# Routed experts in units of two tiles and one, with a row list summed from one-hot tiles

## The chip, the cores and the metric
The kernel runs on one core of a Trainium2 chip. The metric is the device time of one execution in microseconds; the median of three runs before the change is 2113.64 us (2112.92 to 2113.86).

## What is computed
A block of two layers on x of 1 x 2048 x 512 in float32. Layer 0 is a recurrent time mixing, multiplied by the silu of a feed-forward with 2 experts of which each token takes one; layer 1 is a grouped attention (16 heads, 4 key heads, remote keys pooled in blocks of 64, the last 256 kept), multiplied by the silu of a mixture of experts: two shared ones and the best 4 of 16 routed ones for each token. The part that the change touches:

```python
# attention of layer 1
probs = jax.nn.softmax(scores, axis=-1)
out = jnp.einsum('bhqk,bhkd->bhqd', probs, v2)
# mixture of layer 1
scores = jax.nn.sigmoid(flat @ centroids.T) + bias
vals, idx = jax.lax.top_k(scores, KR)                      # KR = 4 of 16
gating = jnp.zeros_like(scores).at[jnp.arange(T)[:, None], idx].set(vals)
gating = gating / jnp.clip(gating.sum(-1, keepdims=True), 1e-08)
hj = jax.nn.relu(flat @ w1 + b1)                           # per expert, 512 -> 352
yj = hj @ w2 + b2                                          # 352 -> 512
acc + yj * g[:, None]
```

## The kernel before
The program is a row of stages, each a block in which the five engines run their own instruction streams and meet by semaphores; between two stages all engines meet. Every product is made in three passes: an operand is kept as a high part (fp32r, cast by ScalarE) and a low part (the rest, subtracted by VectorE or POOL), and TensorE sums high x high, low x high and high x low (`PASSES`). In order of time the stages from layer 1 on are the shared experts with the router, keys and values, window, routed experts, attention.

**Shared experts and router** (`shared_experts_stage` L172, `top4_router` L1587). Eight steps k (two experts x four blocks of 512 tokens). TensorE runs hidden(k), the router's piece of the step, then down(k-1). POOL subtracts the low half of the hidden tiles (L229). VectorE adds the results to y (L272) and runs the router: scores, rank and gates in steps 0 to 3, the places of the tokens in the sorted order (`places`, L1681) in step 4, the shares (L1704) in step 5. From step 5 on POOL scatters (`scatter`, L1770): the 2048 x 4 choices are 64 columns of 128 tokens, and one indirect DMA writes one column of token numbers to their places in the list `idx` in device memory, 32 of them in this stage.

**Keys and values** (`keys_values_stage` L2076). POOL clears the key tiles (L2164), then adds the rotated halves of the keys of block b (L2169), and after each of the four adds scatters eight more columns. VectorE subtracts the weights' low half (L2221), multiplies for the rotation (`rotate`, L2231 and L2232), pools the keys (L2237), and prepares the pooled keys (L2265). TensorE runs `geo_block` 0 and 1, the values, `geo_block` 2 and 3 (L2291), and then places the pooled keys with narrow matmuls of 32 columns (L2325). SP loads raw_o and raw_q, weights of the attention output and query, for the next stage.

**Window** (`window_stage` L2343). Eight units u of window attention. VectorE: `shift(u)` (maxima, L2628), `probs_low(u-1)` (low halves of the turned probabilities, L2662 and L2667), `inverse(u)` (sums and reciprocals, L2644 to L2655). ScalarE: `exps(u)`, `probs_high(u-1)`, `probs(u)`. TensorE: `turn(u)`, then `scores(u+2)`, and `attend` behind every second.

**Routed experts** (`routed_experts_stage` L1789). The sorted list is cut into MT = 47 units of 256 rows (MR), each of one expert. The units run in a loop of two (`tiles`, L1842). SP loads a unit's w1 (two raw buffers) and w2 (one raw buffer, `raw2`) and stores the result y. POOL copies the unit's two columns of indices (L1900), adds on a carrier (L1903), gathers two tiles of 128 rows (L1905) and subtracts w1's low half (L1911). ScalarE casts the high halves (w1 L1936, x L1941, w2 L1950), makes the relu from PSUM into `h32` (L1956) and casts the hidden tile (L1959). VectorE subtracts w2's low half (L1985), the hidden tile's (L1988), the rows' (L1970), and copies y (L1978). TensorE in each unit: 36 hidden matmuls of 256 columns (L2036), 8 transposes of the next unit's rows (L2009), 18 matmuls of the down product of the unit before (L2019). At the stage's start the index list is loaded, turned on TensorE (L2025) and copied by VectorE (L1980) before the first gather.

**Attention** (`attention_stage` L2817). One step of each engine's stream per tile n of 128 queries. TensorE:

```python
if n < NR: geo_query(n)
if 0 <= n - 1 < NR: turn_q(n - 1)
if 0 <= n - 2 < NR: turn_p(n - 2)      # transposes of the probabilities, L3103
if 0 <= n - 1 < NR: scores(n - 1)      # L3113, L3117, then L3122
if 0 <= n - 2 < NR: output(n - 2)      # L3132
```

`turn_p` waits for VectorE's normalised probabilities (att_p, L3016), which follow its maximum (att_mx, L2999) of the scores of that tile.

## Time and profile before

| | |
|---|---|
| median of three runs | 2113.64 us |
| profiled execution, its own time | 2117.64 us |
| its span, first to last instruction | 2115.8 us |
| mean granted clock of TensorE | 0.921 |
| TensorE / VectorE / ScalarE / POOL busy | 85% / 58% / 39% / 49% |
| shared experts and router | 1048.0 to 1238.2 us |
| keys and values | to 1313.5 us |
| window | to 1448.4 us |
| routed experts | to 1911.9 us |
| attention | to 2115.8 us |

Times are microseconds from the span's start. The busy shares are means over stages with different limits, so a stage is read by its own stretch. A matmul's duration reaches beyond the start of the next one, since they overlap; the distance of two starts tells the rate. "[3.39 <-POOL shared_h1l L229]" behind an instruction is the idle time of its engine before it and what ended that. The clock is TensorE's granted clock as a share of 2.4 GHz.

### The profile page before, as it was taken

What the parts mean: (1) busy time and instruction counts of PE and PEld (TensorE: products, weight loads), DVE (VectorE), ACT (ScalarE), POOL (GpSimd) and SP (SyncE); (2) the same over time, 40 slices, a digit from 0 to 9 for tenths busy, and PEclk for the clock granted to TensorE, in tenths of its full rate; (3) what the DMA queues carried; (4) which work ended last, traced back from release to release, by engine and by line L of the source; (5) the groups of instructions that cost most, each with busy time, mean ns of one, the idle gap of its engine ahead of it and who ended that gap; (6) DMA issues with size and microseconds to landing.
All of it is one profiled execution on the core that took longest, in us unless ns stands there. A gap on an engine that the chain in (4) does not pass through costs nothing. (4 is left out here: it accounts for less than half of the span.)

```text
span 2115.8 us, 27097 instructions
## 1 busy us (share of the span) xinstructions
PE 1791.7 (85%) x8864; PEld 1412.2 (67%) x8864; DVE 1228.9 (58%) x1820; ACT 830.0 (39%) x1330; POOL 1033.7 (49%) x654
## 2 busy tenths in 40 slices
PE   3299999999999688896479955866999999996996
PEld 2178888888888333342248844655999999995775
DVE  5244545454445488989516523662566666665886
ACT  3233333333332345554232212453666666651121
POOL 0325454545453254455222555214787877754564
PEclk7699999999999899998779976887999999998998
DMA  5533333323233401122580151003888887876564
GB/s 207 207 120 120 103 119 100 123 91 131 90 124 131 155 20 60 63 97 79 196 299 1 51 183 51 1 1 132 281 283 278 281 285 278 281 225 223 179 205 134
DMA packets 106853, 316.80 MB, mean 150 GB/s; under 512 B 14530, under 2 KB 16160, under 8 KB 105504
## 3 DMA queue, kind: packets, MB, share of 16 engines
q1 hardware_dynamic: 89536, 266.07, 36.8%
q0 software_dynamic: 17248, 49.86, 7.0%
q8 instruction: 37, 0.61, 0.1%
q14 instruction: 32, 0.26, 0.0%
HBM read 248.17 MB, written 67.71 MB: 149 GB/s over the span
## 5 line engine op out<-in xcount | busy, mean ns | idle before, releaser
L704 DVE TENSOR_TENSOR rows<-rffn_ps_y,rows 128x512 f32<-128x512 f32 x255 | 172.9, 690 | 126.2 <-PE rffn_ps_y L790 124.1
L630 POOL TENSOR_TENSOR rffn_w0l<-rffn_raw,rffn_w0h 128x1536 fp32r<-128x1536 f32 x15 | 52.7, 3511 | 154.3 <-ACT rffn_w0h L651 154.3
L723 DVE TENSOR_TENSOR rffn_ps_h<-rffn_ps_up,rffn_silu 128x512 f32<-128x512 f32 (+1 forms) x80 | 47.4, 593 | 124.3 <-PE rffn_ps_up L767 124.0
L1905 POOL DMA_INDIRECT moe_x_in<-xn_rows,moe_idx_now x94 | 97.7, 1040 | 21.2 <-issue 14.7
L1911 POOL TENSOR_TENSOR moe_w_0l<-moe_raw,moe_w_0h 128x1536 fp32r<-128x1536 f32 x24 | 84.4, 3515 | 38.5 <-ACT moe_w_0h L1936 38.5
L1911 POOL TENSOR_TENSOR moe_w_1l<-moe_raw,moe_w_1h 128x1536 fp32r<-128x1536 f32 x23 | 80.9, 3516 | 33.1 <-ACT moe_w_1h L1936 33.1
L1978 DVE COPY moe_y<-moe_ps_y 128x512 f32<-128x512 f32 x94 | 64.3, 686 | 51.7 <-PE moe_ps_y L2019 48.7
L677 ACT CAST rffn_hT0h<-rffn_ps_h 128x512 fp32r<-128x512 f32 (+1 forms) x48 | 24.8, 516 | 155.8 <-DVE rffn_ps_h L723 141.1
L2935 POOL DMA_INDIRECT att_rows<-ys,pos x64 | 65.9, 1030 | 40.0 <-POOLq L55 23.1
L630 POOL TENSOR_TENSOR rffn_w4l<-rffn_raw,rffn_w4h 128x1536 fp32r<-128x1536 f32 x16 | 56.1, 3507 | 59.6 <-ACT rffn_w4h L651 59.6
L1985 DVE TENSOR_TENSOR moe_w_0l<-moe_raw,moe_w_0h 128x1536 fp32r<-128x1536 f32 x24 | 59.0, 2457 | 43.2 <-ACT moe_w_0h L1950 43.2
L630 POOL TENSOR_TENSOR rffn_w3l<-rffn_raw,rffn_w3h 128x1536 fp32r<-128x1536 f32 x16 | 56.1, 3506 | 55.6 <-ACT rffn_w3h L651 55.6
L2036 PE MATMUL moe_ps_hidden<-moe_xs0h,moe_w_0h 128*128 128x256 f32 x288 | 81.6, 283 | 1.5 <-DVE moe_xs0l L1970 1.5
L1956 ACT ACTIVATE moe_h<-moe_ps_hidden,moe_b 128x256 f32<-128x256 f32 x141 | 63.2, 471 | 49.2 <-PE moe_ps_hidden L2036 48.6
L2036 PE MATMUL moe_ps_hidden<-moe_xs0h,moe_w_0l 128*128 128x256 f32 x288 | 81.6, 283 | 0.0
L2036 PE MATMUL moe_ps_hidden<-moe_xs0l,moe_w_0h 128*128 128x256 f32 x288 | 81.4, 283 | 0.0
L1985 DVE TENSOR_TENSOR moe_w_1l<-moe_raw,moe_w_1h 128x1536 fp32r<-128x1536 f32 x23 | 51.5, 2241 | 50.6 <-ACT moe_w_1h L1950 47.5
L2036 PE MATMUL moe_ps_hidden<-moe_xs1h,moe_w_1h 128*128 128x256 f32 x276 | 77.4, 280 | 2.5 <-issue 2.5
L1460 PE MATMUL mix_ps_k<-mix_mix,mix_w 128*128 128x512 f32 x128 | 61.8, 629 | 20.6 <-DVE mix_mix L1146 17.0
L2036 PE MATMUL moe_ps_hidden<-moe_xs1h,moe_w_1l 128*128 128x256 f32 x276 | 77.3, 280 | 0.0
L2036 PE MATMUL moe_ps_hidden<-moe_xs1l,moe_w_1h 128*128 128x256 f32 x276 | 77.0, 279 | 0.0
L1526 PE MATMUL mix_ps_ro<-mix_w,mix_wkv 128*128 128x512 f32 x128 | 62.5, 644 | 16.2 <-POOL mix_wkv L1074 14.9
(716 smaller groups left out, 6260.9 us busy)
## 6 DMA issues: line engine op xcount, KB each, us to landing
rffn_raw<-in_ffn_w SPq DMA_DIRECT2D x80, 768.0 KB, 4.3
moe_raw<-in_moe_w SPq DMA_DIRECT2D x47, 769.5 KB
moe_raw<-in_moe_w SPq DMA_DIRECT2D x47, 768.0 KB, 4.6
ys<-moe_y SPq DMA_DIRECT2D x47, 512.0 KB
xs<-route_zero SPq DMA_DIRECT2D x17, 256.0 KB
rffn_x_in<-xs SPq DMA_DIRECT2D x17, 256.0 KB, 2.8
ys<-rows SPq DMA_DIRECT2D x17, 256.0 KB, 2.1
rows<-in_x SPq DMA_DIRECT2D x4, 1024.0 KB
```

The source lines that it names most:

```text
L630: nc.gpsimd.tensor_tensor(w[b][LO][:], raw[m % 2][:], f32(w[b][HI][:]), ALU.subtract).then_inc(s_w, 1)
L704: nc.vector.tensor_tensor(y[:, t, :], yb[g % 2][:], y[:, t, :], ALU.add).then_inc(s_yadd, 1)
L723: nc.vector.tensor_tensor(hp[:, cols], ub[n % 2][:, cols], sil[n % 2][:, cols], ALU.mult)\
L1460: last = nc.tensor.matmul(bank[:], w[m][:, k, c * P:(c + 1) * P], mix[m][:, k, :], start=(k == 0), stop=(k == KC - 1))
L1526: last = nc.tensor.matmul(ro[t % 2][:], wkv[b % 2][:, k, t * P:(t + 1) * P], w[O_][:, k, :], start=(k == 0), stop=(k == KC - 1))
L1905: nc.gpsimd.indirect_dma_start(out=x_in[j][tt][:], out_offset=None, in_=xn_dram, in_offset=bass.IndirectOffsetOnAxis(ap=now[j][:, tt:tt + ...
L1911: nc.gpsimd.tensor_tensor(w1[j][LO][:], raw1[j][:, 0:W1], f32(w1[j][HI][:]), ALU.subtract).then_inc(s_w1, 1)
L1956: nc.scalar.activation(h32[f][:], hb[f][:], ACT.Relu, bias=b1[j][:, f:f + 1]).then_inc(s_h32, 1)
L1978: nc.vector.tensor_copy(y[:, tt, :], yb[tt][:]).then_inc(s_yc, 1)
L1985: nc.vector.tensor_tensor(w2[j][LO][:], raw2[:], f32(w2[j][HI][:]), ALU.subtract).then_inc(s_w2, 1)
L2036: last = nc.tensor.matmul(hb[f][:], w1[j][p][:, col:col + P], xs[j][q][:, c, :], start=(c == 0 and n == 0), stop=(c == KC - 1 and n == 2))
L2935: nc.gpsimd.indirect_dma_start(out=rows[k % 2][s][:], out_offset=None, in_=ys_dram, in_offset=bass.IndirectOffsetOnAxis(ap=keep.pos4[:, s, ...
```

## The change
**Row list.** The scatters go. The router keeps the places as float numbers (`row4`), in one more step: `bases` in step 4, `places` in step 5, the shares in step 6, with some more small VectorE operations for the singles. In the keys stage VectorE works out for each choice the tile and the row in it, and then makes 64 pairs of one-hot tiles (`one_hots`): 128 x 128 of the row, and 128 x 79 of the tile multiplied by the token number. TensorE sums their 64 fp32 products in one PSUM tile (`token_list`), which is the list of all 79 tiles. The pairs have 16 buffers in raw_o, whose load moves behind the last product. They stand in lots of 24, 20 and 20: ahead of the weights' low half and `geo_block(0)`, behind `geo_block(0)`, behind `geo_block(1)`. VectorE copies the list to SBUF, where it stays.

**Routed experts.** The sorted list is cut into 31 pairs of tiles and 17 singles (`MP`, `MS`; 79 tiles against 94): an expert's last tile stands alone where its count of tiles is odd. The 48 units follow in the order of `MKINDS`, in a loop of six. In a single each operation on rows is made for 128 instead of 256. w2 has two raw buffers and is loaded two units ahead, xs has one buffer, the relu is made in place in PSUM (so hidden(f) waits for VectorE's low part s_h), POOL gathers before it splits, and ScalarE's and VectorE's operations of a unit interleave.

**Window.** VectorE: `inverse(u)`, `shift(u+1)`, `probs_low(u-1)`; ScalarE likewise; TensorE: `scores(u+2)` ahead of `turn(u)`.

**Attention.** `scores(n-1)` without its last 12 matmuls goes ahead of `turn_p(n-2)`, those (`geo_scores`) stay behind it.

```diff
--- before.py
+++ after.py
...
-            env.sync_fill(sp)
...
-                env.pool_step(pool, k)
...
-                link(nc.vector.tensor_reduce(red[:], prod, AX.X, ALU.add))
-                nc.vector.tensor_copy(keep.pos4[:, s, :], red[:]).then_inc(s_pos, 1)
-                dve.wait_ge(s_pos, s + 1)
+                link(nc.vector.tensor_reduce(keep.row4[:, s, :], prod, AX.X, ALU.add))
...
+                bases(dve)
+            if k == 5:
                 places(dve)
-            if k == 5:
+            if k == 6:
...
-        def scatter(pool, n):
-            s, t = n // NT, n % NT
-            return nc.gpsimd.indirect_dma_start(
-                out=idx_dram, out_offset=bass.IndirectOffsetOnAxis(ap=keep.pos4[:, s, t:t + 1], axis=0),
-                in_=keep.ids[:, t:t + 1], in_offset=None)
...
-MT = T * 4 // MR + 15
+MP, MS = 31, 17
+MU = MP + MS
+MG = 2 * MP + MS
...
+MKINDS = [2, 2, 1] * 14 + [2, 1] * 3
+MCYC = 6
...
-        raw2 = a.sb("raw2", [P, W2])
+        raw2 = [a.sb(f"raw2_{j}", [P, W2]) for j in range(2)]
...
-        xs = [[a.sb(f"xs{j}{'hl'[s]}", [P, KC, MR], F32R) for s in (HI, LO)] for j in range(2)]
-        h32 = [a.sb(f"h32_{f}", [P, MR]) for f in range(MF)]
+        xs = [a.sb(f"xs{'hl'[s]}", [P, KC, MR], F32R) for s in (HI, LO)]
...
+        def units(eng, run):
+
+            for m in range(MCYC):
+                run(0, m)
+            with eng.Fori(1, MU // MCYC - 2) as i:
+                for m in range(MCYC):
+                    run(i, m)
+            for m in range(2 * MCYC):
+                run(MU // MCYC - 2, m)
...
+            for m in range(2):
+                src = weights_of(A["moe_w2"], 0, m)
+                sp.dma_start(raw2[m][:], src).then_inc(s_raw2[m], 16)
+
+            def run(i, m):
+                if exists(i, m + 2):
+                    src = weights_of(A["moe_w1"], i, m + 2)
+                    wait(sp, s_w1, number(i, m) + 1)
+                    sp.dma_start(raw1[m % 2][:], src).then_inc(s_raw1[m % 2], 16)
+                if exists(i, m + 2):
+                    src = weights_of(A["moe_w2"], i, m + 2)
+                    wait(sp, s_w2, number(i, m) + 1)
+                    sp.dma_start(raw2[m % 2][:], src).then_inc(s_raw2[m % 2], 16)
...
-            pool.wait_ge(s_idx, 1)
...
+                    gather(i, m + 2)
+                if exists(i, m + 1):
+                    split(i, m + 1)
...
+                relu(0)
+                relu(1)
+                high_h(0)
+                relu(2)
+                high_h(1)
+                if exists(i, m + 1):
+                    high_x(i, m + 1)
+                high_h(2)
...
-                    wait(pe, s_h32, MF * (s - 1) + f + 1)
+                    wait(pe, s_h, MF * (s - 1) + f + 1)
+                            last = nc.tensor.matmul(hb[f][:, 0:cols], w1[j][p][:, col:col + P], xs[q][:, c, 0:cols],
...
+HOT = 16
+WHOLE = 1.5 * 2.0 ** 23
+HOTS = (24, 44, 64)
...
+        hot = keep.raw_o[:, 0:HOT * (P + MG)].rearrange("p (n k) -> p n k", n=HOT)
+        slots = keep.raw_o[:, 3328:3328 + P + MG]
+        at_row = keep.raw_o[:, 3584:3584 + 4 * NT]
+        at_tile = keep.raw_o[:, 3648:3648 + 4 * NT]
+        listed = bL[:].rearrange("p a g k -> p (a g k)")[:, 0:MG]
...
+            sp.wait_ge(s_list, 4 * NT)
+            sp.dma_start(keep.raw_o[:], A["att_o"].rearrange("p c n -> p (c n)")).then_inc(s_pre, 16)
...
-                for n in range(32 + 8 * b, 32 + 8 * b + 8):
-                    keep.scatter(pool, n).then_inc(s_scat, 16)
-            pool.wait_ge(s_scat, 16 * 32)
...
+            def one_hots(first, last):
+                for n in range(first, last):
+                    if n >= HOT:
+                        dve.wait_ge(s_list, n - HOT + 1)
+                    nc.vector.tensor_scalar(hot[:, n % HOT, 0:P], slots[:, 0:P], at_row[:, n:n + 1], None, ALU.is_equal)
+                    nc.vector.tensor_scalar(hot[:, n % HOT, P:P + MG], slots[:, P:P + MG], at_tile[:, n:n + 1],
+                                            keep.ids[:, n % NT:n % NT + 1], ALU.is_equal, ALU.mult).then_inc(s_hot, 1)
+            one_hots(0, HOTS[0])
             dve.wait_ge(s_whi, 1)
...
+            one_hots(HOTS[0], HOTS[1])
             rotate(0)
+            one_hots(HOTS[1], HOTS[2])
             rotate(1)
             pool_keys(0)
+            dve.wait_ge(s_list, 4 * NT)
+            nc.vector.tensor_copy(keep.idx[:], listed).then_inc(s_idx, 1)
...
+            def token_list(first, last):
+                for n in range(first, last):
+                    pe.wait_ge(s_hot, n + 1)
+                    nc.tensor.matmul(listed, hot[:, n % HOT, 0:P], hot[:, n % HOT, P:P + MG],
+                                     start=(n == 0), stop=(n == 4 * NT - 1)).then_inc(s_list, 1)
+            token_list(0, HOTS[0])
             pe.wait_ge(s_w, 1)
             geo_block(0)
+            token_list(HOTS[0], HOTS[1])
             geo_block(1)
+            token_list(HOTS[1], HOTS[2])
...
+            exps(0)
             for u in range(2 * HKV):
-                exps(u)
-                if u:
-                    probs_high(u - 1)
                 probs(u)
+                if u + 1 < 2 * HKV:
+                    exps(u + 1)
+                probs_high(u)
                 if u >= 3 and u % 2:
                     out_high((u - 3) // 2)
-            probs_high(2 * HKV - 1)
...
+            shift(0)
             for u in range(2 * HKV):
-                shift(u)
+                inverse(u)
+                if u + 1 < 2 * HKV:
+                    shift(u + 1)
                 if u:
                     probs_low(u - 1)
-                inverse(u)
...
-                turn(u)
                 if u + 2 < 2 * HKV:
                     scores(u + 2)
+                turn(u)
...
+            def geo_scores(i):
+                out = sb_[i % 2]
...
+                if 0 <= n - 1 < NR:
+                    scores(n - 1)
                 if 0 <= n - 2 < NR:
                     turn_p(n - 2)
                 if 0 <= n - 1 < NR:
-                    scores(n - 1)
+                    geo_scores(n - 1)
```

TensorE's instructions of one steady tile of attention, before (L3095 turns the queries, L3103 the probabilities):

```order
L3095 MATMUL att_ps_qT<-att_ident,att_q 128x128 x4
L3103 MATMUL att_ps_pT<-att_ident,att_p 128x128 x4
L3113 MATMUL att_ps_scores<-att_madd,att_ident_r 128x512
L3117 MATMUL att_ps_scores<-folded_q,att_xq2h 128x512 x2
L3117 MATMUL att_ps_scores<-folded_q,att_xq2l 128x512
...
L3117 MATMUL att_ps_scores<-folded_q,att_xq2l 128x512
L3122 MATMUL att_ps_scores<-kqh,att_qTh 128x128
L3122 MATMUL att_ps_scores<-kql,att_qTh 128x128
L3122 MATMUL att_ps_scores<-kqh,att_qTl 128x128
```

and now, where L3195, L3203, L3213 and L3217 are those of L3095, L3103, L3113 and L3117:

```order
L3195 MATMUL att_ps_qT<-att_ident,att_q 128x128 x4
L3213 MATMUL att_ps_scores<-att_madd,att_ident_r 128x512
L3217 MATMUL att_ps_scores<-folded_q,att_xq2h 128x512 x2
L3217 MATMUL att_ps_scores<-folded_q,att_xq2l 128x512
...
L3217 MATMUL att_ps_scores<-folded_q,att_xq2l 128x512
L3203 MATMUL att_ps_pT<-att_ident,att_p 128x128 x4
L3225 MATMUL att_ps_scores<-kqh,att_qTh 128x128
L3225 MATMUL att_ps_scores<-kql,att_qTh 128x128
```

The transposes of the probabilities stood ahead of all score matmuls and stand now between those on folded_q and the narrow ones.

POOL's instructions of two units of the routed experts, before:

```order
L1911 TENSOR_TENSOR moe_w_1l<-moe_raw_1,moe_w_1h 128x1536
L1900 COPY moe_idx_now<-moe_idx 128x2
L1903 TENSOR_TENSOR moe_carrier<-moe_carrier 128x1
L1905 DMA moe_x_in<-xn_rows,moe_idx_now 128x512 x2
L1911 TENSOR_TENSOR moe_w_0l<-moe_raw_0,moe_w_0h 128x1536
L1900 COPY moe_idx_now<-moe_idx 128x2
L1903 TENSOR_TENSOR moe_carrier<-moe_carrier 128x1
L1905 DMA moe_x_in<-xn_rows,moe_idx_now 128x512 x2
```

and now, two pairs and a single:

```order
L1946 COPY moe_idx_now<-token_list 128x2
L1949 TENSOR_TENSOR moe_carrier<-moe_carrier 128x1
L1951 DMA moe_x_in<-xn_rows,moe_idx_now 128x512 x2
L1958 TENSOR_TENSOR moe_w_0l<-moe_raw_0,moe_w_0h 128x1536
L1946 COPY moe_idx_now<-token_list 128x2
L1949 TENSOR_TENSOR moe_carrier<-moe_carrier 128x1
L1951 DMA moe_x_in<-xn_rows,moe_idx_now 128x512 x2
L1958 TENSOR_TENSOR moe_w_1l<-moe_raw_1,moe_w_1h 128x1536
L1946 COPY moe_idx_now<-token_list 128x1
L1949 TENSOR_TENSOR moe_carrier<-moe_carrier 128x1
L1951 DMA moe_x_in<-xn_rows,moe_idx_now 128x512
```

The gathers stand ahead of the split of the next unit, and the last unit shown copies one column of indices and gathers one tile.

VectorE's instructions at the start of the keys stage, before:

```order
L2216 TENSOR_SCALAR kv_bar<-xn_sums 128x4x28
L2217 TENSOR_REDUCE kv_bar<-xn_sums 128x4
L2218 TENSOR_SCALAR kv_bar<-kv_bar 128x4
L2219 MEMSET kv_geo 128x32
L2221 TENSOR_TENSOR kv_wl<-kv_raw,kv_wh 128x2560
L2223 TENSOR_TENSOR kv_barl<-kv_bar,kv_barh 128x512
L2231 TENSOR_TENSOR kv_t_0<-kv_ps_k,kv_rope 128x512
```

and now (24 pairs of L2300 and L2301 ahead of L2305):

```order
L2285 CAST pos<-row 128x64
L2286 TENSOR_SCALAR raw_o<-row 128x64
L2288 TENSOR_SCALAR raw_o<-raw_o 128x64
L2290 TENSOR_SCALAR raw_o<-raw_o 128x64
L2292 SCALAR_TENSOR_TENSOR raw_o<-raw_o,row 128x64
L2300 TENSOR_SCALAR raw_o<-raw_o 128x128
L2301 TENSOR_SCALAR raw_o<-raw_o,ids 128x79
...
L2300 TENSOR_SCALAR raw_o<-raw_o 128x128
L2301 TENSOR_SCALAR raw_o<-raw_o,ids 128x79
L2305 TENSOR_TENSOR kv_wl<-kv_raw,kv_wh 128x2560
L2307 TENSOR_TENSOR kv_barl<-kv_bar,kv_barh 128x512
L2300 TENSOR_SCALAR raw_o<-raw_o 128x128
```

Ahead of the weights' low half (L2221 before, L2305 now) stand five small operations and 48 one-hot ones; on TensorE 24 matmuls of 79 columns stand ahead of `geo_block(0)`.

## Rows read from the trace of the kernel before

**Rows 1.** Stages: start:end and us, then the columns of the first line
```profile
core 0: us, PE busy (x) PEld busy (x) DVE busy (x) ACT busy (x) POOL busy (x), PEclk, DMA share, GB/s
1313.50:1448.40 134.90, 96.08 (x504) 82.63 (x504) 73.12 (x134) 54.70 (x120) 19.90 (x12) 0.83 0.07 24
1464.30:1911.90 447.60, 440.37 (x2906) 400.56 (x2906) 278.90 (x374) 287.07 (x512) 332.60 (x226) 0.99 0.78 267
1500.00:1900.00 400.00, 399.57 (x2657) 363.71 (x2656) 252.41 (x342) 262.77 (x468) 303.60 (x207) 1.00 0.81 276
1295.00:1306.00 11.00, 10.07 (x48) 10.10 (x48) 0.72 (x4) 0.22 (x1) 7.36 (x8) 0.50 0.02 2
```

**Rows 2.** Timeline of TensorE, one routed unit: start us, us, instruction
```profile
1605.24 0.28 PE L2036 MATMUL moe_ps_hidden<-moe_xs1h,moe_w_1h 128*128 128x256 f32 x1
...
1609.49 1.03 PE L2009 MATMUL moe_ps_x<-moe_ident,moe_x_in 128*128 128x128 f32 x8
1610.28 0.48 PE L2019 MATMUL moe_ps_y<-moe_w_0h,moe_h0h 128*128 128x512 f32 x1
...
1614.56 0.28 PE L2036 MATMUL moe_ps_hidden<-moe_xs0h,moe_w_0h 128*128 128x256 f32 x1
```

**Rows 3.** Groups, routed stage (busy us, mean ns, idle before), and POOL's timeline
```profile
L1905 POOL DMA_INDIRECT moe_x_in<-xn_rows,moe_idx_now x90 | 93.8, 1042 | 20.1 <-issue 13.8
...
L1956 ACT ACTIVATE moe_h<-moe_ps_hidden,moe_b 128x256 f32<-128x256 f32 x141 | 63.2, 471 | 49.2 <-PE moe_ps_hidden L2036 48.6
...
L1941 ACT CAST moe_xs1h<-moe_ps_x 128x512 fp32r<-128x512 f32 x46 | 24.8, 594 | 0.0
...
1613.88 3.51 POOL L1911 TENSOR_TENSOR moe_w_1l<-moe_raw,moe_w_1h 128x1536 fp32r<-128x1536 f32 x1 [0.85 <-ACT moe_w_1h L1936]
```

**Rows 4.** Attention: TensorE's timeline, and one of its waits (us, times, longest)
```profile
2009.52 0.28 PE L3122 MATMUL att_ps_scores<-kql,att_qTh 128*128 128x128 f32 x1
...
2010.63 0.28 PE L3122 MATMUL att_ps_scores<-kqh,att_qTl 128*128 128x128 f32 x1
...
2017.50 0.66 PE L3103 MATMUL att_ps_pT<-att_ident,att_p 128*128 128x128 f32 x4 [0.52 <-DVE att_p L3016]
...
PE att_ps_pT L3103 <- DVE att_p L3016: 20.9, 14, 6.2
```

**Rows 5.** Timelines of TensorE, VectorE and POOL, end of the shared experts
```profile
1218.65 0.50 PE L300 MATMUL shared_ps_y<-shared_w1h,shared_h1h 128*128 128x512 f32 x1 [3.39 <-POOL shared_h1l L229]
...
1227.30 0.69 DVE L272 TENSOR_TENSOR y<-shared_ps_y,y 128x512 f32<-128x512 f32 x1 [1.46 <-PE shared_ps_y L300]
...
1238.20 0.31 POOL L2164 MEMSET kbdh<- 128x256 f32 x1 [5.69 <-POOLq L55]
```

**Rows 6.** Timelines, keys stage (VectorE, TensorE), then TensorE's fp32 counts
```profile
1238.38 0.22 DVE L2216 TENSOR_SCALAR kv_bar<-xn_sums 128x112 f32<-128x112 f32 x1
...
1238.84 1.78 DVE L2218 TENSOR_SCALAR kv_bar<-kv_bar 128x4 f32<-128x4 f32 x1
...
1249.23 0.79 PE L2291 MATMUL kv_ps_k<-xn1h,kv_wh 128*128 128x512 f32 x1 [22.09 <-DVE kv_wl L2221]
...
1295.93 0.36 PE L2325 MATMUL kv_ps_placed<-kv_kph,kv_sel 128*128 128x32 f32 x1 [13.39 <-DVE kv_kpl L2265]
...
1173.38 0.59 PE L1754 MATMUL shared_ps_counts<-shared_sel,shared_consts 128*128 128x256 f32 x2
1173.82 0.59 PE L1756 MATMUL shared_ps_counts<-shared_sel,shared_ones 128*128 128x256 f32 x2
```

**Rows 7.** One line's instructions (ns), and VectorE's timeline, window stage
```profile
L2653 DVE RECIPROCAL win_winv<-win_ssum x8: 178/178/179, 1367.8 to 1424.4; 128x4 f32<-128x4 f32 x8
...
1371.92 1.29 DVE L2662 TENSOR_TENSOR win_wqs_pw<-win_ps_x,win_wqs_pw 128x512 fp32r<-128x512 f32 x2 [1.99 <-ACT win_wqs_pw L2537]
```

**Rows 8.** Timeline of POOL, start of the routed stage
```profile
1452.26 0.18 POOL L1900 COPY moe_idx_now<-moe_idx 128x2 uint32<-128x2 uint32 x1 [3.68 <-DVE moe_idx L1980]
```

369 lines of the change are left out of this document (198 added, 171 removed).

## Prediction

> **What bounds the kernel now.** I read the stage table first [rows 1]. The routed experts take 447.6 us, and in 400 us of their middle TensorE is busy 399.57 us at full clock: whatever shortens its work there shortens the kernel. The window stage is different: TensorE is busy 96.08 of 134.90 us at a granted clock of 0.83, so a chain through ScalarE and VectorE sets it. Then I read TensorE's timeline of one routed unit [rows 2], what the other engines do in a unit [rows 3], and, for the stages before and behind, the waits and the steps that follow each other [rows 4 to 8]. The sum below is made against the profiled execution (2117.64 us, span 2115.8), which is 4.0 us above the median of 2113.64; I take these 4.0 off at the end. A difference of 0.2%, some 4 us, is about what a measurement of this kernel can tell from no change.
>
> **Routed units, the large term.** A unit of two tiles [rows 2]: 36 hidden matmuls from 1605.24 to 1609.49 (4.25 us, 0.118 each), 8 transposes to 1610.28 (0.79), 18 down matmuls to 1614.56 (4.28): 9.32 us, and 47 of them are 438.0. Now there are 31 such pairs and 17 singles. A single issues the same 36 hidden matmuls on 128 columns, half of the transposes and half of the down matmuls. Its hidden part doesn't halve: the twelve 128-column matmuls of one attention tile follow each other at 0.111 us (ten steps from 2009.52 to 2010.63 [rows 4]), hardly faster than those of 256 columns. So a single costs 36 x 0.111 + 0.40 + 2.14 = 6.54 us, and the stage 31 x 9.32 + 17 x 6.54 = 400.1: **-37.9**, though 79 tiles stand for 94. Two things could take from it. xs has one buffer now, so the next unit's tiles are cast and split while TensorE does the transposes and a down part; behind a single that is only 0.79 + 2.14 = 2.93 us, and the way through ScalarE (the last relu 0.47, two casts of 0.59 and one more of a hidden block [rows 3]) and VectorE's last subtraction is about as long. I count no stall, and 0.25 us in each of 17 (+4) for the range. And POOL: it is busy 303.60 us in 43 units [rows 1], 7.06 a unit, of which one gather of 1.04 falls away in a single [rows 3]: 6.0 and its short issue gaps, within 6.54, and POOL waited 0.85 us for ScalarE in a pair [rows 3]. It is close, and the second buffer for w2 lets loads run two units ahead. Ends: -30 with both stalls, -42 if the hidden part shrinks to 3.7 us.
>
> TensorE's rate there has a rule in the Trainium skill ("TensorE: Matmul & The Clock Gate", section "Back-to-back issue gap"): streams of weight load and matmul settle at about 81 ns each for 128 columns. The 0.111 us of the row is higher; by the page this term would be some 18 us larger (a rival below).
>
> **Start of the routed stage.** POOL's first index copy waits 3.68 us for the index list that is loaded, turned on TensorE and copied [rows 8]; now the list lies in SBUF, and the gathers start about 4 us earlier. The split of the first weights stands behind them on POOL and is earlier by as much, until it waits for ScalarE's half. **-4**, from -2 (weights late) to -6.
>
> **End of the shared experts.** 32 scatters go from POOL. TensorE's last down part waited 3.39 us for POOL's low half of the hidden tile, which was queued behind scatters; the next stage's first instruction comes at 1238.20, 5.69 us after the last scatter's end, while the last sum was done at 1227.99 [rows 5]. Without them the last sum ends near 1224.6, its store and the stage's change need some 4 to 5 us: 1229. **-9**; -3.5 if the router's extra small VectorE operations hold up the sums, -10 at best.
>
> **Keys stage.** 32 scatters go from POOL, 64 one-hot pairs come to VectorE and 64 fp32 matmuls to TensorE, in lots of 24, 20 and 20. The first lot stands on both engines ahead of everything: VectorE makes 24 pairs and only then subtracts the weights' low half, for which TensorE's first key matmul waited until 1249.23 [rows 6]. A pair costs at least two operations of the kind of 0.22 us (112 columns) and at most 1.78 us more where POOL's memsets run, as the 4-column one at 1238.84 took [rows 6]. At 0.35 a pair, 24 are 8.4 us from about 3.5 us into the stage, and the key matmuls start 6.5 later (3 to 12). A one-hot matmul is fp32 with 79 columns: the counts matmuls of 256 columns took 0.44 us each [rows 6], of which 79 columns are a third (0.14), and half the clock or the weight load would give 0.43. I take 0.213, the pitch that narrow matmuls show at half clock, [rows 1] 10.07 us for 48: 40 of them in line are +8.5 (5.5 to 17). Against that stands the wait of 13.39 us at 1295.93 [rows 6]: TensorE waits there for a chain through POOL's rotation adds, each of which stood behind eight scatters. With an idle POOL the chain is two VectorE products, an add and a sum, about 4.4 us: -9. The three together: **+6**, between -5 and +14. The 2 MB load of raw_o moves behind the last one-hot matmul on SP's queue; it has more than 20 us until the stage's end, which covers it; without this cover it would cost its own 8 us.
>
> **Window stage.** The eight units are 8.09 us apart ((1424.4 - 1367.8) / 7 [rows 7]). VectorE did probs_low(u-1) between shift(u) and inverse(u), and there it first waited 1.99 us for ScalarE and then worked 1.29 us and more while the sum of the unit stood behind it [rows 7]. In the new order inverse(u) and shift(u+1) come first. The chain through exps, sums and reciprocals keeps its own length, so not all of these 3.3 us go: I count about a quarter, 0.75 in each of eight units, since ScalarE's operations follow in nearly the same order as before: **-6**, from 0 (the chain closes through TensorE's transposes instead) to -18.
>
> **Attention stage.** TensorE waits 20.9 us in 14 places for VectorE's probabilities before it transposes them (20.9, 14, 6.2 [rows 4]); in a steady tile that is 0.52 us. Ahead of this wait stand now the 13 score matmuls of 2.8 us, and turn_p comes after. That hides the steady 0.5 us of ten tiles (5 us) and in the four others, the first and last ones, where the remaining 15.7 us of waiting lie (6.2 the longest), up to 2.8 us each (about 10). From the 20.9 I take **-15**; what is late next is VectorE's low half of the turned probabilities, which had the score matmuls as its cover. Ends -8 and -18 (nothing above 20.9 can come).
>
> **Sum**: -37.9 - 4 - 9 + 6 - 6 - 15 = -66, so 2051.6 profiled and **2047.6** as the median.
>
> **Rivals.**
> 1. The one-hots cost what the window was to give: keys +14 and window 0 (VectorE is the bound at the keys' start, as the 1.78 us row threatens). -66 + 8 + 6 = -52: 2061.6. For it speaks that the first lot stands ahead of the weights.
> 2. A single is not bound by TensorE but by transfers or POOL. A unit of 2.6 MB in 9.32 us moved at 276 GB/s with a DMA share of 0.81 [rows 1]; a single still loads both weights and moves 2.08 MB. 31 x 2.6 + 17 x 2.08 = 116 MB at 276 GB/s is 420 us, 20 more than the forecast: 2068. Against it: the share of 0.81 leaves room, and TensorE, not DMA, ended the waits.
> 3. The hidden matmuls of a single run at 0.081 us: 36 x 0.030 x 17 = 18 us less, 2029. This is the page's figure named above. Against it speaks the row at 0.111, the same kind of operand at full clock.
> 4. Slower. The granted clock falls to 1.2 GHz in the singles and comes back only after them. It fell to 0.50 while 48 narrow matmuls of 32 columns ran for 11 us, though TensorE and its weight loads were busy 10.07 and 10.10 us of them [rows 1]. A single at half clock costs 6.54 more, all 17 of them 111 us: 2047.6 + 111 = 2159. It decides from 66 / 6.54 = 10 singles of 17. Against it: 128-column matmuls between wide ones ran at full clock in attention.
> The Trainium skill ("TensorE: Matmul & The Clock Gate", section "Why this matters for your kernels") warns of it for fewer than 512 rows, where it wants padding or another loop; the attention rows don't show it, and no run here shows a single.
>
> **How the numbers follow.** Forecast 65%, rival 1 14%, rival 2 10%, rival 3 5%, rival 4 6% (4 with most singles, 2 with about ten of them, which comes out as no change). The terms' bounds (-99 to -30 in sum, against -66) won't all fall to one side: half of the distance is some 17 us each way. Rivals 1 to 3 lie at 2029 to 2068; with a few us of the terms' own spread on either side the range is 2022 to 2073. Faster by over 0.2%: 0.94; within 0.2%: 0.02; slower: 0.04.
>
> **What would show it.** In the profile of the changed kernel: 36 narrow hidden matmuls in about 4.0 us and a stage of about 410 us from the first hidden matmul on, at a clock near 1; keys' first matmul 6 to 7 us later in its stage, the wait ahead of the placed matmuls under 5 us; reciprocals about 7.3 us apart; no wait of TensorE for the probabilities in steady attention, tiles 11.1 us apart. Wrong would be: a granted clock under 0.9 in the routed stage, a pitch of singles above 7.5 us, POOL or DMA as what ends TensorE's waits there, or a stage of keys longer by over 14 us.

## The result, and the profile after

The changed kernel takes 2083.02 us (median of four runs, 2077.27 to 2083.78) against 2113.75 before: a ratio of 0.9846, with a 95% interval of 0.9825 to 0.9866. It is faster, by 30.7 us where 66 were forecast, and lies outside the range of 2022 to 2073. The profiled execution took 2083.04 us (span 2081.2), so it sits on the median; the 4.0 us by which the profile of before lay above its own median belonged to that one execution. The kernel before was run again in each later series, with medians of 2114.6 to 2116.3 us. One execution of u_att took 6222 us, three times as long as the others, and is left out of its median. In spans the change is 2115.8 to 2081.2, or -34.6 us.

The stages, each from its first instruction to that of the next, in us (the shared experts' first instruction before is at 1054.49, not at the 1048.0 of the earlier table):

| stage | before | changed | difference | forecast |
|---|---|---|---|---|
| all ahead of the shared experts | 1054.5 | 1056.1 | +1.6 | 0 |
| shared experts and router | 183.7 | 173.5 | -10.2 | -9 |
| keys and values | 75.4 | 85.6 | +10.2 | +6 |
| window | 134.9 | 132.1 | -2.8 | -6 |
| routed experts | 464.2 | 438.7 | -25.5 | -41.9 |
| attention | 203.1 | 195.2 | -7.9 | -15 |

Two stages hold the miss: 16.4 us in the routed experts and 7.1 in attention; keys and window add 4.2 and 3.2. The stage table of the changed kernel, which answers to [rows 1] (start:end, us, then the columns of the first line):

```profile
core 0: us, PE busy (x) PEld busy (x) DVE busy (x) ACT busy (x) POOL busy (x), PEclk, DMA share, GB/s
1315.20:1447.30 132.10, 94.39 (x504) 82.08 (x504) 73.40 (x134) 54.94 (x120) 19.91 (x12) 0.85 0.07 25
1460.30:1886.00 425.70, 405.31 (x2747) 366.96 (x2747) 317.98 (x348) 267.24 (x506) 294.40 (x212) 0.99 0.76 266
1500.00:1840.00 340.00, 329.89 (x2250) 298.75 (x2248) 259.71 (x286) 219.95 (x416) 248.29 (x181) 1.00 0.81 280
1886.00:2081.20 195.20, 167.70 (x797) 135.63 (x797) 164.13 (x239) 36.05 (x60) 104.88 (x94) 0.91 0.63 195
```

The 340 us in the middle of the routed stage are what to look at. Before, TensorE was busy 399.57 of 400 us; now it is 329.89 of 340, so it has become a waiting engine. The DMA share and the rate are the same as before (0.81, 280 against 276 GB/s), and the clock is full.

TensorE's timeline of a pair and of the single behind it, which answers to [rows 2]:

```profile
1600.64 0.39 PE L2088 MATMUL moe_ps_hidden<-moe_xsh,moe_w_0h 128*128 128x256 f32 x1 [1.34 <-DVE moe_xsl L2023]
...
1609.63 0.22 PE L2088 MATMUL moe_ps_hidden<-moe_xsh,moe_w_1h 128*128 128x128 f32 x1
...
1613.60 1.06 PE L2061 MATMUL moe_ps_x<-moe_ident,moe_x_in 128*128 128x128 f32 x8
1614.41 0.48 PE L2072 MATMUL moe_ps_y<-moe_w_0h,moe_h0h 128*128 128x512 f32 x1
```

The single's hidden part runs from 1609.63 to 1613.60, 3.97 us for 36 matmuls or 0.110 each, as the attention row of 0.111 had said. The Trainium skill ("TensorE: Matmul & The Clock Gate", section "Back-to-back issue gap") gives some 81 ns for 128 columns; here it is 110 ns. The price of a single was right, then. What wasn't in it is the idle 1.34 us ahead of the hidden part of the pair at 1600.64. The waits from 1465 to 1865 us (us in total, times, longest); before, the same window had no wait of TensorE for the rows' low parts (the middle line) and 2.5 us of the last kind:

```profile
ACT moe_b L1980 <- DMA moe_raw<-in_moe_w: 96.4, 44, 3.5
...
PE moe_ps_hidden L2088 <- DVE moe_xsl L2023: 9.7, 9, 1.5
...
PE moe_ps_hidden L2088 <- issue: 4.3, 4, 1.8
```

ScalarE waits 96.4 us for the loads of w1. Such a wait alone costs nothing: before, it waited 81.7 us in the same window for the loads of w1 and w2 (25.4, 33.2 and 23.1), and TensorE had next to no gap. The way of one such load, in the timelines of POOL, SP, ScalarE and VectorE:

```profile
1602.28 3.52 POOL L1958 TENSOR_TENSOR moe_w_1l<-moe_raw,moe_w_1h 128x1536 fp32r<-128x1536 f32 x1 [0.94 <-ACT moe_w_1h L1981]
...
1610.71 0.41 SPq L1936 DMA_DIRECT2D ys<-moe_y  x1
1612.03 0.33 SPq L1923 DMA_DIRECT2D moe_raw<-in_moe_w  x1
...
1618.28 0.20 ACT L1980 COPY moe_b<-moe_raw 128x3 f32<-128x3 f32 x1 [2.77 <-DMA moe_raw<-in_moe_w]
...
1619.93 3.51 POOL L1958 TENSOR_TENSOR moe_w_1l<-moe_raw,moe_w_1h 128x1536 fp32r<-128x1536 f32 x1 [3.23 <-ACT moe_w_1h L1981]
...
1621.27 3.80 DVE L2037 TENSOR_TENSOR moe_w_0l<-moe_raw,moe_w_0h 128x1536 fp32r<-128x1536 f32 x1 [1.68 <-ACT moe_w_0h L1997]
...
1625.65 1.27 DVE L2023 TENSOR_TENSOR moe_xsl<-moe_ps_x,moe_xsh 128x512 fp32r<-128x512 f32 x2
```

POOL is done with the w1 buffer at 1602.28 + 3.52 = 1605.80. SP issues the load into it at 1612.03, 6.2 us later: its queue is in order, and ahead of this load stood the load of w2 and the store of y, which waited for VectorE's copy until 1610.71. The data are there at 1618.28, where ScalarE has waited 2.77 us. Behind ScalarE's casts POOL subtracts from 1619.93 on, and VectorE's operation on w2, begun at 1621.27, lasts 3.80 us where the shortest ones took 1.76. Only then come the low parts of the rows at 1625.65, for which TensorE waits. From one subtraction to the next in the same buffer (1602.28 to 1619.93) it takes 17.65 us, and TensorE's work in two average units is 16.7 (400.1 / 48, twice). There were two suspects, then: the late load, and VectorE's slow operation.

The end of the shared experts, which answers to [rows 5], shows its term as forecast: last sum at 1225.92 + 0.69, next stage 3 us after it, without a scatter between them.

```profile
1225.92 0.69 DVE L270 TENSOR_TENSOR y<-shared_ps_y,y 128x512 f32<-128x512 f32 x1 [1.35 <-PE shared_ps_y L298]
...
1229.59 0.31 POOL L2230 MEMSET kbdh<- 128x256 f32 x1 [14.91 <-POOLq L55]
```

The keys stage, which answers to [rows 6] (its first instruction is at 1229.59):

```profile
1236.00 1.10 DVE L2300 TENSOR_SCALAR raw_o<-raw_o 128x128 f32<-128x128 f32 x1
1236.20 0.94 DVE L2301 TENSOR_SCALAR raw_o<-raw_o,ids 128x79 f32<-128x79 f32 x1
...
1240.52 0.27 DVE L2300 TENSOR_SCALAR raw_o<-raw_o 128x128 f32<-128x128 f32 x1
1240.71 0.31 DVE L2301 TENSOR_SCALAR raw_o<-raw_o,ids 128x79 f32<-128x79 f32 x1
...
1240.65 9.25 PE L2400 MATMUL kv_ps_placed<-raw_o 128*128 128x79 f32 x42 [0.30 <-DVE raw_o L2301]
...
1251.90 0.80 PE L2379 MATMUL kv_ps_k<-xn1h,kv_wh 128*128 128x512 f32 x1 [2.00 <-DVE kv_wl L2305]
...
1297.63 0.36 PE L2423 MATMUL kv_ps_placed<-kv_kph,kv_sel 128*128 128x32 f32 x1 [5.34 <-issue]
```

While POOL clears the key tiles, a pair of one-hots takes 1.0 to 1.4 us; from 1240.52 on it takes 0.42. TensorE's 42 records from 1240.65 on are 21 products, one each 0.42 us, which is the pace of VectorE's pairs. The first key matmul starts 22.3 us into its stage; before it was 11.0. The wait ahead of the placed matmuls shrank from 13.39 to 5.34 us.

The window's reciprocals, which answer to [rows 7], are (1417.6 - 1370.9) / 7 = 6.67 us apart where they were 8.09:

```profile
L2751 DVE RECIPROCAL win_winv<-win_ssum x8: 177/178/178, 1370.9 to 1417.6; 128x4 f32<-128x4 f32 x8
```

Attention, which answers to [rows 4], VectorE's and POOL's timelines of a steady tile, and then TensorE's waits for the probabilities and for their low half:

```profile
1978.01 0.68 DVE L3099 TENSOR_REDUCE att_mx<-att_ps_scores 128x16 f32<-128x512 f32 x1
...
1983.62 2.17 DVE L3116 TENSOR_TENSOR att_p<-att_p,att_inv 128x512 f32<-128x512 f32 x1
...
1989.49 0.68 DVE L3099 TENSOR_REDUCE att_mx<-att_ps_scores 128x16 f32<-128x512 f32 x1
...
1983.93 1.30 POOL L3048 TENSOR_TENSOR att_res<-att_res,att_x_in 128x512 f32<-128x512 f32 x1
```

```profile
PE att_ps_pT L3203 <- DVE att_p L3116: 7.1, 3, 3.2
...
PE att_ps_out L3235 <- DVE att_pTl L3174: 4.4, 11, 1.4
```

The wait fell from 20.9 to 7.1 us as meant, but the tiles are 11.48 us apart (1978.01 to 1989.49) where 11.1 were forecast and 11.58 stood before. TensorE waits in nearly every tile for the low half of the turned probabilities instead (the last line; before, 1.4 us in one place). VectorE is busy 11.02 of the 11.48 us, where it was busy 9.81 of 11.58 before, and the rest are gaps of 0.12 us at most between its operations. Its product of the probabilities (L3116, two SBUF operands) took 2.17 us instead of 0.93: POOL's residual add began at 1983.93, just behind it, and ran 1.30 us.

### The profile page after: what moved, and what is told of

It reads as the page before. It is cut to its first block and busy times, and to the rows that moved or that the text cites. A ratio compares the mean times of both kernels' runs of the same rounds, so it can differ in the third digit from the quotient of the medians.

```text
span 2081.2 us, 26247 instructions
## 1 busy us (share of the span) xinstructions
PE 1779.8 (86%) x8832; PEld 1402.0 (67%) x8832; DVE 1315.1 (63%) x1938; ACT 811.0 (39%) x1324; POOL 933.6 (45%) x578
## 5 line engine op out<-in xcount | busy, mean ns | idle before, releaser
L2037 DVE TENSOR_TENSOR moe_w_1l<-moe_raw,moe_w_1h 128x1536 fp32r<-128x1536 f32 x24 | 88.8, 3702 | 44.6 <-ACT moe_w_1h L1997 44.6
L2037 DVE TENSOR_TENSOR moe_w_0l<-moe_raw,moe_w_0h 128x1536 fp32r<-128x1536 f32 x24 | 91.7, 3819 | 34.5 <-ACT moe_w_0h L1997 34.5
L2088 PE MATMUL moe_ps_hidden<-moe_xsh,moe_w_0h 128*128 128x256 f32 (+1 forms) x288 | 81.7, 284 | 8.6 <-DVE moe_xsl L2023 6.6
L2088 PE MATMUL moe_ps_hidden<-moe_xsh,moe_w_1h 128*128 128x256 f32 (+1 forms) x288 | 80.2, 279 | 7.4 <-DVE moe_xsl L2023 4.6
L2088 PE MATMUL moe_ps_hidden<-moe_xsl,moe_w_0h 128*128 128x256 f32 (+1 forms) x288 | 81.1, 282 | 0.0
L2088 PE MATMUL moe_ps_hidden<-moe_xsh,moe_w_0l 128*128 128x256 f32 (+1 forms) x288 | 81.0, 281 | 0.0
L2088 PE MATMUL moe_ps_hidden<-moe_xsh,moe_w_1l 128*128 128x256 f32 (+1 forms) x288 | 79.9, 278 | 0.0
L2088 PE MATMUL moe_ps_hidden<-moe_xsl,moe_w_1h 128*128 128x256 f32 (+1 forms) x288 | 79.9, 277 | 0.0
L1458 PE MATMUL mix_ps_v<-mix_mix,mix_w 128*128 128x512 f32 x128 | 63.3, 641 | 15.1 <-DVE mix_e2v L1175 15.1
L2002 ACT ACTIVATE moe_ps_hidden<-moe_ps_hidden,moe_b 128x256 f32<-128x256 f32 (+1 forms) x144 | 57.5, 408 | 47.4 <-PE moe_ps_hidden L2088 46.7
```

The source lines that it names most:

```text
L1458: last = nc.tensor.matmul(bank[:], w[m][:, k, c * P:(c + 1) * P], mix[m][:, k, :], start=(k == 0), stop=(k == KC - 1))
L2002: nc.scalar.activation(hb[f][:, 0:n], hb[f][:, 0:n], ACT.Relu, bias=b1[j][:, f:f + 1]).then_inc(s_h32, 1)
L2037: nc.vector.tensor_tensor(w2[j][LO][:], raw2[j][:], f32(w2[j][HI][:]), ALU.subtract).then_inc(s_w2, 1)
L2088: last = nc.tensor.matmul(hb[f][:, 0:cols], w1[j][p][:, col:col + P], xs[q][:, c, 0:cols], start=(c == 0 and n == 0), stop=(c == KC - 1 an ...
```

## The experiments

Each kernel is the changed one with the edit shown, unless it says otherwise. The stage times are from first instruction to first instruction, as above, and each is read from one profiled execution. A ratio is to the kernel before in the same series of runs.

### VectorE's w2 operation later: r_w2late

```diff
             def run(i, m):
-                wait(dve, s_w2hi, s + 1)
-                nc.vector.tensor_tensor(w2[j][LO][:], raw2[j][:], f32(w2[j][HI][:]), ALU.subtract).then_inc(s_w2, 1)
...
                 low_h(2)
+                wait(dve, s_w2hi, s + 1)
+                nc.vector.tensor_tensor(w2[j][LO][:], raw2[j][:], f32(w2[j][HI][:]), ALU.subtract).then_inc(s_w2, 1)
                 if not at_start(i, m):
                     copy_y(i, m - 1)
```

> The changed kernel with one move: in the routed experts VectorE subtracts w2's low half behind the last low half of the hidden tile, not at the unit's start. Theory A (exclusion): VectorE's operation on two SBUF operands doesn't advance while POOL's subtraction of w1 runs, so it took 3.8 us instead of 1.76 and made the next unit's rows late behind each single. Then here L2037's operation takes about 1.8 us, TensorE's idle time of 20 us in the stage falls under 5, and the stage of 438.7 us becomes about 422. Theory B (transfers bound the stage at some 280 GB/s): the stage keeps 435 to 440 us, and ScalarE's waits for the loads stay near 96 us in total. Theory C (ScalarE's and VectorE's own chain behind a short down part is too long whatever overlaps): a third of the gain at most, 432 to 438.

Measured: 2082.86 us (ratio to before 0.9842, 0.9825 to 0.9858), the same as the changed kernel; the routed stage took 442.3 us. A wait of the stage, and VectorE's and SP's timelines:

```profile
ACT moe_b L1980 <- DMA moe_raw<-in_moe_w: 134.0, 42, 6.8
```

```profile
1610.03 1.75 DVE L2046 TENSOR_TENSOR moe_w_0l<-moe_raw,moe_w_0h 128x1536 fp32r<-128x1536 f32 x1
...
1611.95 0.33 SPq L1927 DMA_DIRECT2D moe_raw<-in_moe_w  x1
...
1613.16 0.41 SPq L1936 DMA_DIRECT2D ys<-moe_y  x1
1614.48 0.33 SPq L1923 DMA_DIRECT2D moe_raw<-in_moe_w  x1
```

VectorE's operation is as short as theory A wanted (1.75 us, all 48 of them) and nothing was gained, so a short operation alone is not enough. But the edit moved something else too: w2's buffer is freed later (1610.03 + 1.75), SP waits for that before it issues w2, and the store and w1 come behind it; the wait for loads grew to 134.0 us. So this run neither clears A nor shows it. Theory B seemed to stand.

### Less for POOL, and fewer bytes: r_shortsplit, r_halfload

```diff
-                nc.gpsimd.tensor_tensor(w1[j][LO][:], raw1[j][:, 0:W1], f32(w1[j][HI][:]), ALU.subtract).then_inc(s_w1, 1)
+                c = W1 if isinstance(i, int) and i == 0 and m < 2 else 512
+                nc.gpsimd.tensor_tensor(w1[j][LO][:, 0:c], raw1[j][:, 0:c], f32(w1[j][HI][:, 0:c]), ALU.subtract)\
+                  .then_inc(s_w1, 1)
```

> Leaves work out: from the third unit on POOL subtracts 512 of the 1536 columns of w1's low half, 1.2 instead of 3.5 us; nothing else moves. Theory A: VectorE's w2 operation falls from 3.8 to about 1.8 us and the stage from 438.7 to about 422 us. Theory B: the loads are as many, so the stage stays above 434. Theory C: above 432.

```diff
-                    sp.dma_start(raw1[m % 2][:], src).then_inc(s_raw1[m % 2], 16)
+                    sp.dma_start(raw1[m % 2][:, 0:768], src[:, 0:768]).then_inc(s_raw1[m % 2], 16)
...
-                    sp.dma_start(raw2[m % 2][:], src).then_inc(s_raw2[m % 2], 16)
+                    sp.dma_start(raw2[m % 2][:, 0:768], src[:, 0:768]).then_inc(s_raw2[m % 2], 16)
```

> Leaves work out: from the third unit on the loads of w1 and w2 bring 768 of 1539 and 1536 columns, so the weights' bytes are halved. Theory A: ScalarE's casts come earlier and POOL's and VectorE's operations still collide, w2's operation stays at 3 to 3.8 us and the stage is 432 to 439 us. Theory B: the stage falls to TensorE's work, 420 us or less.

Measured, one execution each: r_shortsplit 2060.3 us with a routed stage of 422.6 us, r_halfload 2058.2 us with 422.3. The stage's middle in r_halfload, then in r_shortsplit:

```profile
core 0: us, PE busy (x) PEld busy (x) DVE busy (x) ACT busy (x) POOL busy (x), PEclk, DMA share, GB/s
1500.00:1840.00 340.00, 340.00 (x2337) 311.42 (x2336) 255.82 (x300) 231.76 (x435) 234.74 (x187) 1.00 0.64 197
...
1500.00:1840.00 340.00, 340.00 (x2344) 311.67 (x2344) 197.99 (x297) 227.93 (x435) 134.23 (x186) 1.00 0.85 291
```

and ScalarE's wait for the loads in r_shortsplit, from 1465 to 1865 us:

```profile
ACT moe_b L1982 <- DMA moe_raw<-in_moe_w: 84.4, 43, 3.3
```

Both reach TensorE's own work, and none of the three theories explains both. r_shortsplit came out as A had said: VectorE's operation fell to 1.76 us and the stage to 422.6. But with half the bytes VectorE's operation still took 3.5 to 3.6 us (medians), and TensorE didn't wait; so A's slow operation alone doesn't cost the time. With all bytes and a short subtraction the rate rose to 291 GB/s, so 280 GB/s was no ceiling; that is against B. What the two have in common is that the way of a w1 load is shorter in one of its steps: landing and cast in one, the subtraction and what it holds up in the other. That led to theory D: the way is too long because its first step, the issue, comes 6 us late on SP's queue.

### The load's place on SP's queue: r_w1early, r_both

```diff
+            src = weights_of(A["moe_w1"], 0, 2)
+            wait(sp, s_w1, 1)
+            sp.dma_start(raw1[0][:], src).then_inc(s_raw1[0], 16)
...
-                if exists(i, m + 2):
-                    src = weights_of(A["moe_w1"], i, m + 2)
-                    wait(sp, s_w1, number(i, m) + 1)
-                    sp.dma_start(raw1[m % 2][:], src).then_inc(s_raw1[m % 2], 16)
+                if exists(i, m + 3):
+                    src = weights_of(A["moe_w1"], i, m + 3)
+                    wait(sp, s_w1, number(i, m) + 2)
+                    sp.dma_start(raw1[(m + 1) % 2][:], src).then_inc(s_raw1[(m + 1) % 2], 16)
```

> The changed kernel with one move on SP's queue in the routed experts: the load of w1 for unit m+3 stands where that of m+2 stood, so it is issued when POOL's subtraction has freed its buffer, and no longer behind the store of the unit before and that one's wait for VectorE's copy. Bytes are the same. Theory D (a late issue: the w1 load waited some 4 to 6 us in SP's queue with its buffer already free, and ScalarE, which waits for it, holds up everything behind): ScalarE's wait for the loads falls from 96 to under 50 us, TensorE's idle time from 20 to under 5 us, the stage from 438.7 to 421 to 426 us. Theory B (the rate of the transfers is the bound): the stage stays within 3 us of 438.7, with the waits at another place. Theory A (only VectorE's blocked operation): w2's operation stays at about 3.8 us and the stage above 434.

Measured: 2062.4 us (0.9751, 0.9734 to 0.9767), routed stage 422.3 us. The stage's middle (columns as above), and POOL's and SP's timelines:

```profile
1500.00:1840.00 340.00, 340.00 (x2339) 311.43 (x2338) 253.21 (x299) 229.36 (x433) 238.31 (x191) 1.00 0.85 291
```

```profile
1597.96 3.51 POOL L1961 TENSOR_TENSOR moe_w_1l<-moe_raw,moe_w_1h 128x1536 fp32r<-128x1536 f32 x1
...
1601.64 0.33 SPq L1926 DMA_DIRECT2D moe_raw<-in_moe_w  x1
...
1606.69 0.41 SPq L1939 DMA_DIRECT2D ys<-moe_y  x1
```

The buffer is free at 1601.47 and the load is issued at 1601.64, with the same bytes and the same number of buffers. TensorE is busy 340.00 of 340 us, ScalarE's wait for the loads is gone from the list, and the rate is 291 GB/s. VectorE's w2 operation still takes 3.5 to 3.6 us in the median. All of theory D's numbers came, none of A's or B's: with the load on time the loss is gone. The stage is 41.9 us shorter than before, as was the forecast of 37.9 + 4; that it fits to a tenth is luck, since the start alone gave 2.8 instead of 4.

> The move of r_w1early together with that of r_w2late. Theory D with A: both lates are gone, stage 420 to 424 us, TensorE busy throughout. Theory D alone: the same as r_w1early within 1.5 us. Theory B: 436 or more.

Measured: 2064.5 us (0.9761, 0.9744 to 0.9778), routed stage 422.2 us, as in r_w1early: once the load is early, the short operation adds nothing.

The late load is not the whole of it, though. In r_shortsplit the load was issued even later after its buffer was free (8.3 us in the median) and ScalarE waited 84.4 us for the loads, and TensorE still was busy 340.00 of 340 us. The loss needs the late load and something behind it that is long, VectorE's blocked operation or POOL's subtraction of 3.51 us; r_shortsplit shortens both, and no run takes these two apart.

### The same move in the kernel before: b_w1early

The kernel before, with this edit:

```diff
+            src = weights_of(A["moe_w1"], 2)
+            wait(sp, s_w1, 1)
+            sp.dma_start(raw1[0][:], src).then_inc(s_raw1[0], 16)
...
-                if after(s, 2):
-                    src = weights_of(A["moe_w1"], s + 2)
-                    wait(sp, s_w1, s + 1)
-                    sp.dma_start(raw1[j][:], src).then_inc(s_raw1[j], 16)
+                if after(s, 3):
+                    src = weights_of(A["moe_w1"], s + 3)
+                    wait(sp, s_w1, s + 2)
+                    sp.dma_start(raw1[1 - j][:], src).then_inc(s_raw1[1 - j], 16)
```

> The kernel before with the move of r_w1early alone. Theory D says that the late issue costs only where the units have become shorter than the way of the load: before, TensorE was busy 399.57 of 400 us, so nothing can come, 2113 to 2116 us. If the load's place had cost something before too, the routed stage would fall below its 464 us.

Measured: 2118.9 us, ratio 1.0007 (0.9991 to 1.0022), routed stage 465.5 us against 464.2. So the load's place cost nothing before, though the load was issued later than it is now; POOL's and SP's timelines of the kernel before:

```profile
1596.21 3.52 POOL L1911 TENSOR_TENSOR moe_w_1l<-moe_raw,moe_w_1h 128x1536 fp32r<-128x1536 f32 x1 [2.12 <-ACT moe_w_1h L1936]
...
1607.55 0.34 SPq L1879 DMA_DIRECT2D moe_raw<-in_moe_w  x1
```

The buffer is free at 1599.73 and the load is issued 7.8 us after that (median of the stage 8.8, and 6.2 in the changed kernel). Two things are new in the changed kernel. Its units are 10% shorter (8.34 us on average against 9.32), and VectorE's w2 operation is blocked in nearly every unit: its median is 3.79 us with 47 of 48 above 3 us, where it was 2.43 with 4 of 47. The even units alone, before and changed (ns, shortest/median/longest):

```profile
L1985 DVE TENSOR_TENSOR moe_w_0l<-moe_raw,moe_w_0h x24: 1758/2450/3769, 1466.3 to 1897.3; 128x1536 fp32r<-128x1536 f32 x24
...
L2037 DVE TENSOR_TENSOR moe_w_0l<-moe_raw,moe_w_0h x24: 3495/3794/4551, 1462.3 to 1864.4; 128x1536 fp32r<-128x1536 f32 x24
```

How much of the 16.4 us belongs to each was not tried.

### POOL's add in attention: a_pooladd, a_pooladd2

```diff
             for n in range(NT + 1):
+                if n >= 1:
+                    result(n - 1)
                 if n < NR:
                     rotated(n)
                 if n + 1 < NT:
                     gather(n + 1)
-                if n >= 1:
-                    result(n - 1)
```

The first try, a_pooladd, had `if n >= 2: result(n - 2)` ahead of `rotated(n)`:

> The changed kernel with one move in attention: POOL adds the block's residual of tile n-2 ahead of the rotated query of tile n, so it no longer falls into VectorE's product of the probabilities with their inverse sums. Theory A: that product (L3116) falls from 2.17 to about 0.7 to 0.9 us, VectorE has 1.3 us of slack a tile, and the tile's period falls from 11.47 to about 11.1 us, TensorE's own work: the stage of 195.2 us becomes 190 to 192. Rival: the period is set by TensorE's work and its wait for the low half (0.3 us) alone, then it moves by under 0.1 us a tile, the stage by under 1.5.

Measured: 2079.2 us (0.9829, 0.981 to 0.9848), L3116's product still 2.17 us, attention 194.7 us. The edit only carried the add from the end of one pass to the start of the next, so POOL's order didn't change. It tells nothing of the rivals, but it is a replica of the changed kernel, 4 us from it: so much can two medians of the same program differ.

> The changed kernel with POOL's residual add of tile n-1 ahead of the rotated query of tile n (in a_pooladd it only went from the end of one pass to the start of the next, which is the same place). It now runs while VectorE works on operands in PSUM. Exclusion: L3116 falls from 2.17 to about 0.7 us, the tile's period from 11.47 to 11.0 to 11.2 us (TensorE's own work), the stage from 195.2 to 190 to 192. Rival: POOL's add blocks VectorE's operations with a PSUM operand just as well, then these grow by 1.3 us and the period stays at 11.47.

Measured: 2074.0 us (0.9809, 0.9789 to 0.9828), attention 190.0 us. VectorE's and POOL's timelines:

```profile
1982.79 0.69 DVE L3099 TENSOR_REDUCE att_mx<-att_ps_scores 128x16 f32<-128x512 f32 x1
...
1988.42 0.69 DVE L3116 TENSOR_TENSOR att_p<-att_p,att_inv 128x512 f32<-128x512 f32 x1
...
1993.98 0.69 DVE L3099 TENSOR_REDUCE att_mx<-att_ps_scores 128x16 f32<-128x512 f32 x1
...
1990.52 1.30 POOL L3048 TENSOR_TENSOR att_res<-att_res,att_x_in 128x512 f32<-128x512 f32 x1 [3.05 <-DVE att_res L3141]
...
1990.96 0.68 DVE L3149 TENSOR_TENSOR att_tt<-att_ps_geo,att_rope 128x512 f32<-128x512 f32 x1
```

The product takes 0.69 us, the tiles are 11.19 us apart, and POOL's add runs from 1990.52 to 1991.82 under operations of VectorE with an operand in PSUM, which keep their 0.68 us (the last line). Against the replica's 2079.2 us the gain is 5.2, as much as the stage became shorter. Exclusion holds, for two SBUF operands. The Trainium skill ("GPSIMD Engine Reference", section "Specifications") says that POOL's SBUF interfaces are shared with VectorE, with contention for instructions with two SBUF inputs; the trace agrees, and here the contention is a standstill: the product takes 1.48 us longer when POOL's add of 1.30 runs in it.

### Lots of the one-hot pairs: k_lots

```diff
-HOTS = (24, 44, 64)
+HOTS = (2, 18, 34, 49, 64)
...
             pool_keys(0)
-            dve.wait_ge(s_list, 4 * NT)
-            nc.vector.tensor_copy(keep.idx[:], listed).then_inc(s_idx, 1)
+            one_hots(HOTS[2], HOTS[3])
...
+            one_hots(HOTS[3], HOTS[4])
             rotate(2)
             pool_keys(1)
+            dve.wait_ge(s_list, 4 * NT)
+            nc.vector.tensor_copy(keep.idx[:], listed).then_inc(s_idx, 1)
...
+            token_list(HOTS[2], HOTS[3])
             geo_block(2)
+            token_list(HOTS[3], HOTS[4])
```

> The changed kernel with the one-hot pairs of the keys stage in five lots of 2, 16, 16, 15 and 15 where three of 24, 20 and 20 stood: only two stand ahead of the weights' low half, and the last two lots stand behind the third block of keys on TensorE. If the lot in front is what made the stage 10.2 us longer, the first key matmul comes about 12 us into the stage instead of 22.3 and the stage falls from 85.6 to 76 to 79 us. Rival: VectorE's pairs, 0.42 us each, hold TensorE up wherever they stand; then the stage stays above 82 us.

Measured: 2078.6 us (0.9818, 0.9795 to 0.9842), keys 80.2 us. The stage began at 1232.00, and TensorE's first key matmul:

```profile
1243.76 0.79 PE L2381 MATMUL kv_ps_k<-xn1h,kv_wh 128*128 128x512 f32 x1 [2.01 <-DVE kv_wl L2305]
```

It stands 11.8 us into the stage, 10.5 earlier than in the changed kernel, and the stage is 5.4 shorter: 80.2 us, between the 76 to 79 expected and the 82 of the rival. The other half of the 10.5 didn't come through, and why was not tried. The window behind it took 134.1 us against 132.1; u_att below, with the window and the keys untouched, took 135.0, so this need not come from the lots. The kernel's time of 2078.6 is no clear gain: the replica above had 2079.2.

### The orders undone: u_att, u_win

The edits put back the orders of the kernel before: attention's (shown), and in the window stage those of VectorE (shown), ScalarE and TensorE.

```diff
-                if 0 <= n - 1 < NR:
-                    scores(n - 1)
                 if 0 <= n - 2 < NR:
                     turn_p(n - 2)
+                if 0 <= n - 1 < NR:
+                    scores(n - 1)
                 if 0 <= n - 1 < NR:
                     geo_scores(n - 1)
```

```diff
-            shift(0)
             for u in range(2 * HKV):
-                inverse(u)
-                if u + 1 < 2 * HKV:
-                    shift(u + 1)
+                shift(u)
                 if u:
                     probs_low(u - 1)
+                inverse(u)
```

> The changed kernel with attention's order as before: all score matmuls behind turn_p. The stage was 203.1 us before and is 195.2 now; undone it should be 202 to 204 us, 7 to 9 us slower than the changed kernel, if the new order alone brought that and nothing came from the other stages. With the score matmuls behind the transposes VectorE's blocked product (2.17 us) should be gone or shorter, since it starts at another time than POOL's add, as before (0.93).

Measured: 2082.8 us (three executions; 0.9843, 0.9819 to 0.9866), attention 200.8 us; the probabilities' product is back at 0.92 us, TensorE's wait for it at 19.9 us, and the tiles 11.57 us apart. By the stage the order is worth 5.6 of the 7.9 us. The kernel's time doesn't show it: 2082.8 is level with the changed kernel's 2083.0, where 7 to 9 us more were expected, and 5.6 us is hardly more than two series of one program differ by. The other 2.3 lie in the first tiles; b_w1early, whose attention is that of the kernel before, took 201.6 us for it instead of 203.1, so 1.5 of them may be no effect at all. The product's 0.92 isn't undisturbed either: POOL's add runs into its first 0.37 us.

> The changed kernel with the window stage's orders as before on VectorE, ScalarE and TensorE. The stage was 134.9 us before and is 132.1 now. If the order brought the 2.8 us, it is 134 to 136 us here and the kernel 2 to 4 us slower; if they came from elsewhere, it stays at 132.

Measured: 2085.6 us (0.9862, 0.9841 to 0.9883), window 135.5 us, reciprocals 8.17 us apart. The order is worth 3.4 us in the stage, which with 2.6 us in the kernel's time is as expected, but within what two series differ by; the pace of the reciprocals is the firmer sign.

### All three moves: best

It is r_w1early, a_pooladd2 and k_lots together.

> The changed kernel with the three moves that answered: w1's load one unit sooner on SP's queue, POOL's residual add ahead of the rotated query, and five lots of one-hot pairs. Each acts in another stage, so the gains should add: routed experts 422 us, attention 190 us, keys 80 us, against 438.7, 195.2 and 85.6: 27 us less than the changed kernel, 2083.0 - 27 = 2056 us or a few less (two replicas of the changed kernel lay 4 us apart). If a stage's gain is given back by a neighbour (raw_o's load comes later and holds up the window stage), the sum is 2062 or more.

Measured: 2052.8 us (five runs), ratio to before 0.9706 (0.9687 to 0.9725): 30 us faster than the changed kernel. Routed experts 422.5 us, attention 188.9, keys 79.6, window 133.3. That is 3 us below the 2056 expected. The window's 1.2 us more than in the changed kernel is less than runs with the same window code differ by (131.5 to 135.0).

## Why the prediction was right or wrong

**Routed experts: wrong by 16.4 us, and the size of the work was right.** 31 pairs at 9.32 and 17 singles at 6.54 us stood as computed, for with the load moved the stage fell by 41.9 us, and two pairs and a single took 8.9, 9.1 and 7.2 us, 25.2 in all, as 2 x 9.32 + 6.54 had said. The step that failed is the bound: "I count no stall, and 0.25 us in each of 17". I had only asked whether each engine's busy time fits in a unit's 6.54 us, and whether ScalarE's and VectorE's way behind a short down part does. The way of a w1 load through SP's queue I never followed; I counted the second w2 buffer as a help. What the runs showed in its place: the load was issued 6.2 us after its buffer was free, VectorE's w2 operation took 3.79 us instead of 1.76, and TensorE waited for what came behind them; with the load issued on time the 16.4 us were gone. The load had been late before as well (8.8 us in the median) and cost nothing there, so it is the way as a whole, held against the shorter units, that was missing from the sum. For SP's queue the diff shows nothing that would catch the eye, since the order stands there as before. Rival 2 (2068) had the place and a size of 20 us; its mechanism, a rate of 276 GB/s that can't be exceeded, was wrong, since the same bytes flow at 291 GB/s in r_w1early.

**Start of the routed stage.** Forecast -4, measured -2.8: the first hidden matmul comes 13.0 us into the stage and came 15.8 into it.

**Attention: -7.9 instead of -15.** TensorE's wait went as forecast (20.9 to 7.1). The sentence "what is late next is VectorE's low half of the turned probabilities, which had the score matmuls as its cover" named the right wait: TensorE now waits for it 4.4 us in 11 places. What failed is that the -15 put no price on it. The low half is late because VectorE is full, busy 11.02 us of a tile's 11.48, and 1.25 of these are new: the product took 2.17 us under POOL's add and 0.92 before. It is the new order that brought the two together, since without it (u_att) the product takes 0.92. With the add moved the stage is 13.1 us shorter than before.

**Keys: +10.2 instead of +6, within its bounds.** The 40 products between the blocks cost 0.22 us each (0.213 taken), the wait fell by 8.0 (9 taken). The start was mis-sized: 11.3 us later, not 6.5. A pair costs 0.42 us and not 0.35, and under POOL's memsets 1.0 to 1.4; of the five small operations ahead of them four took 0.9 to 1.6 each. The three terms as measured (+11.3, +8.8, -8.0) make 12.1 and the stage grew by 10.2; the other 1.9 were not followed. The upper bound of 12 had this in it, from the row of 1.78 us; the value I took didn't.

**Window: -2.8 instead of -6.** The units drew together by more than I said, 8.09 to 6.67 us, some 10 us in all. But the first reciprocal comes 1.5 us later in its stage, and from the last one to the stage's end it takes 29.7 us where it took 24.1. I summed over the loop and didn't look at its two ends.

**Shared experts: -10.2 against -9.** Right, by its own steps.

**The 4.0 us** taken off for the profiled execution belonged to that execution, not to the kernel; without this the forecast would have been 2051.6. It makes up 4.0 of the 35.4 us between forecast and result, the terms the other 31.4.

**Rivals.** Rival 1 (2061.6) came in part: keys +10.2 of its +14, window -2.8 instead of 0. Rival 3 (2029) didn't come: the hidden matmuls of a single took 0.110 us. Nor did rival 4, the slower one: the singles ran at full clock (1.00 in the stage's middle).

## What to carry to other kernels

When units get shorter, follow the way of each transfer once around: buffer free, issue, landing, cast, last reader, and hold it against the new distance of the units. The issue is a step of its own, and on an in-order queue it waits for everything ahead of it; a place that cost nothing (b_w1early) cost 16 us once the units were 10% shorter and VectorE's operation behind it was blocked. And ahead of moving an operation on VectorE with two SBUF operands, look at what POOL does at the new time.

## What the runs showed of the hardware

VectorE's operations on two SBUF operands stood still while POOL's operation ran. The 128 x 1536 subtraction takes 1.76 us alone and 3.80 when POOL's of 3.51 us runs for its first 2.2; the 128 x 512 product 0.69 us alone and 2.17 when POOL's add of 1.30 starts in it. Operations with one operand in PSUM kept their 0.68 us under the same add. The one-hot compares, with one SBUF tensor and a scalar, were held up by POOL's memsets as well: 128 x 128 took 0.27 us after the last memset and 1.05 to 1.47 before. It also goes the other way: POOL's copy of 128 x 2 numbers took 1.69 us under VectorE's w2 operation and 0.18 without it.

```profile
1447.47 0.18 POOL L1946 COPY moe_idx_now<-token_list 128x2 uint32<-128x2 uint32 x1
...
1605.77 1.69 POOL L1946 COPY moe_idx_now<-token_list 128x2 uint32 x1
```
